# Rebalancing GpSimd's triangular inverse over four steps and moving two short scans, in a gated delta-rule layer

## The reference, cut to what matters

```python
qkvz = hidden_states @ W_qkvz
...
conv = sum((xp[:, j:j + Tv, :] * conv_w[:, j] for j in range(CONV_K)))   # 4 taps
conv = _silu(conv)
...
def step(S, inp):
    q_t, k_t, v_t, a_t, b_t = inp
    S = S * a_t[..., None, None]
    err = jnp.einsum('bhkv,bhk->bhv', S, k_t)
    v_new = (v_t - err) * b_t[..., None]
    S = S + k_t[..., None] * v_new[..., None, :]
    o = jnp.einsum('bhkv,bhk->bhv', S, q_t)
    return (S, o)
...
og = o * _silu(z)
og = og * jax.lax.rsqrt(jnp.mean(og * og, axis=-1, keepdims=True) + EPS) * norm_weight
return og.reshape(Bv, Tv, VDIM) @ W_out
```

## Time and profile before

| | us |
|---|---|
| median of 3 runs (lowest to highest) | 1186.12 (1184.61 to 1191.84) |
| the profiled execution's own time | 1186.36 |
| its span | 1184.6 |
| PE busy | 1085.0 (92%) |
| DVE busy | 931.3 (79%) |
| ACT busy | 801.6 (68%) |
| POOL busy | 740.0 (62%) |
| mean granted PE clock | 0.973 |

### The profile page before, as it was taken

The page is one execution under the profiler, slowest core; times in us unless marked ns, Lnnn a source line. Parts: engine busy times, 40 slices in busy tenths (PEclk is TensorE's granted clock), DMA queues, the critical chain, the costliest instruction groups (busy, mean ns, idle before and its releaser), DMA issues. The chain is left out here.

```text
span 1184.6 us, 29919 instructions
## 1 busy us (share of the span) xinstructions
PE 1085.0 (92%) x10488; PEld 950.3 (80%) x10488; DVE 931.3 (79%) x2531; ACT 801.6 (68%) x2225; POOL 740.0 (62%) x1183
## 2 busy tenths in 40 slices
PE   7885999999999999999999999999989878998985
PEld 6784898889888888988888989888878767776653
DVE  6898798999999898989899999999872534328754
ACT  6442687777777787877777777778675764229883
POOL 3166778787878778787878787877867412015111
PEclk9778899999999999999999999999998999999998
DMA  5222227314040413222231404041224130010000
GB/s 190 66 61 49 76 58 70 89 38 119 15 110 18 111 39 86 56 70 60 69 89 38 118 15 111 17 109 22 61 45 123 35 107 1 1 62 16 2 19 19
DMA packets 140869, 72.79 MB, mean 61 GB/s; under 512 B 114184, under 2 KB 130064, under 8 KB 138800
## 3 DMA queue, kind: packets, MB, share of 16 engines
q1 hardware_dynamic: 140720, 70.88, 23.9%
HBM read 57.06 MB, written 13.78 MB: 60 GB/s over the span
## 5 line engine op out<-in xcount | busy, mean ns | idle before, releaser
L1084 POOL TENSOR_TENSOR Tn<-Tn,tmp 64x31 f32<-64x31 f32 (+15 forms) x496 | 279.3, 563 | 38.9
L1081 POOL TENSOR_TENSOR tmp<-DT,Tn 64x31 f32<-64x31 f32 (+15 forms) x496 | 251.5, 507 | 50.6 <-DMA DT<-blk_in_scratch 11.9
L878 DVE SCALAR_TENSOR_TENSOR cv<-bank,cw,cv 128x255 f32<-128x255 f32 (+2 forms) x384 | 155.0, 472 | 42.2 <-ACT cv L674 41.6
L878 DVE SCALAR_TENSOR_TENSOR cqk<-bank,cw,cqk 128x255 f32<-128x255 f32 (+2 forms) x384 | 154.8, 471 | 35.3 <-ACT cqk L674 35.3
L1052 POOL TENSOR_TENSOR ro<-ss,mhalf 128x4 f32<-128x4 f32 x64 | 72.4, 1132 | 143.5 <-issue 75.9
L935 DVE SCALAR_TENSOR_TENSOR BP<-bank,cj,E 128x512 f32<-128x512 f32 (+1 forms) x256 | 144.5, 610 | 2.5 <-DVE cj L916 0.3
L485 PE MATMUL bank<-wo,OTs 128*128 128x256 f32 x512 | 137.3, 396 | 1.5 <-ACT OTs L767 1.5
L744 ACT ACTIVATE ogn<-og,ro 128x128 f32<-128x128 f32 x256 | 82.1, 401 | 38.8 <-POOL ro L1052 38.8
L736 ACT ACTIVATE junk<-og 128x129 f32<-128x129 f32 x256 | 79.4, 310 | 36.9 <-issue 25.9
L485 PEld LDWEIGHTS bank<-wo,OTs 128*128 128x128 f32 x512 | 89.5, 192 | 13.9 <-ACT OTs L767 2.0
L464 PE MATMUL bank<-Y,BP 128*128 128x128 f32 x512 | 88.6, 275 | 0.1
(11 more groups left out here) (212 smaller groups left out, 3256.1 us busy)
## 6 DMA issues: line engine op xcount, KB each, us to landing
rvz<-in_L_attn_W_qkvz SPq DMA_DIRECT2D x16, 512.0 KB, 5.4
x<-alpha_scratch SPq DMA_DIRECT2D x8, 1024.0 KB, 5.0
alb<-alpha_scratch SPq DMA_DIRECT2D x7, 1024.0 KB, 5.0
rqk<-in_L_attn_W_qkvz SPq DMA_DIRECT2D x16, 256.0 KB, 2.6
wo<-in_L_attn_W_out SPq DMA_DIRECT2D x16, 256.0 KB
blk_in_scratch<-BP SPq DMA_DIRECT2D x256, 16.0 KB, 1.5
DT<-blk_in_scratch SPq DMA_DIRECT2D x16, 256.0 KB, 3.4
tinv_scratch<-Tn SPq DMA_DIRECT2D x32, 128.0 KB, 2.2
```

Of the source, the lines that this page charges most:

```text
L878: nc.vector.scalar_tensor_tensor(d, bk[:, t * T:(t + 1) * T - s], cw[p][:, first + t, TAPS - 1 - s:TAPS - s], d, ALU.mult, ALU.add).then_i ...
L1081: pool_step_done(nc.gpsimd.tensor_tensor(t, D[:, j, j + 1:BLK].unsqueeze(2).broadcast_to([SLOTS, r, c]), T[:, j, 0:c].unsqueeze(1).broadca ...
L1084: pool_step_done(nc.gpsimd.tensor_tensor(T[:, j + 1:BLK, 0:c], T[:, j + 1:BLK, 0:c], t, ALU.subtract), t_rows(kh, j + 1))
```

## The change

Two edits, both in the loop. POOL's 31 rows are dealt 14, 3, 7, 7 over the four steps in place of 16, 3, 7, 5: rows 14 and 15 leave step 0, and step 3 ends with rows 24 to 30 in place of 26 to 30. On DVE, in step 2, the two short scans (L892) move from in front of the q/k taps to behind them, which is in front of the v taps; the long scan stays in front. (From here on lines in the changed kernel are 2 higher: L1081 becomes L1083.)

```diff
                     elif b == 2:
-                        scans_ahead(1, 1)
+                        scans_ahead(1, 1, R)
                 for taps in (taps_v, taps_qk) if merges(b) else (taps_qk, taps_v):
                     for n in range(1, TAPS):
                         taps(n)
+                    if b == 2 and taps == taps_qk:
+                        scans_ahead(1, R)
...
-            SPLIT = ((0, 16), (16, 19), (19, 26), (26, BLK - 1))
+            SPLIT = ((0, 14), (14, 17), (17, 24), (24, BLK - 1))
```

## The result

| | before | after |
|---|---|---|
| median (lowest to highest), us | 1185.55 (1184.61 to 1191.84), 4 runs | 1212.19 (1210.81 to 1213.38), 4 runs |
| ratio, 95% interval | | 1.021 (1.018 to 1.025) |
| profiled execution: own time, span | 1186.36, 1184.6 | 1210.81, 1209.1 |
| mean granted PE clock there | 0.973 | 0.954 |

The account below looks back on a forecast made before the run. PE was the first suspect, with the chain to `UT` arriving at about the same time. Gains of 1.85 against later v side, inverse and landing gave +0.2 a round, +3 us in 13 rounds: 1189 us, range 1176 to 1203.

Parts of the forecast that it names:

- edit 1 up to PE: Rows 14 and 15 leave step 0, so `ogn` starts 1.85 us earlier and PE's wait at L475 goes almost entirely.
- the sum for a round: From one L409 to the next: +0.28 us in odd rounds, +0.15 in even ones, mean +0.2.
- My 1.08 less 0.40: Transposed inverse issued 1.08 us sooner behind the first issue, less 0.40 for slower landing of `UT` when issues crowd.
- The rivals with faster blocks: Blocks keep up, both PE waits go: 1160 us, chance 0.11; or landings as short as the median: 1179, chance 0.15.
- The one with throughput: DMA traffic fixes the time from first issue to `UT` landing: about +1.0 us a round, 1200 us, chance 0.18.
- edit 2: Short scans behind the q/k taps in step 2: PE's wait at L333 goes, v taps and squares of step 2 come later.
- my two terms: Delay of the v side in step 2 from moving the scans: 0.37 us in odd rounds, 0.94 in even ones.
- The step that failed: PE, ready some 2 us earlier each round, waits that long for the blocks at L399 or L409.
- A second step: The gain in front of L475 was counted in rounds 1 to 13 only; the first and last two got none.
- 1.16 us: In step 3 the transposed inverse leaves this much later, seen from the squares of step 2, after the later last row.

Follow-up runs that it names:

- edit 1 alone: Kernel before with POOL's rows dealt 14, 3, 7, 7 and the short scans left in front of the q/k taps: 1196.15 us, ratio 1.010.
- the best dealing: Kernel before with POOL's rows dealt 15, 4, 7, 5, one row moved from step 0 to step 1: 1167.96 us, ratio 0.987.
- the two fillers: Changed kernel with ten useless matmuls a round before the wait for `U`: 1207.90 us; with eight more before the wait for `UT`: 1203.03 us.
- edit 2 alone: Kernel before, dealing 16, 3, 7, 5 kept, with step 2's two short scans moved behind the q/k taps: 1192.37 us, ratio 1.006.
- raw blocks last: Changed kernel with SP's read of raw blocks moved behind the transposed inverse out: 1212.09 us, ratio 1.024 to the kernel before.

## Why the prediction was wrong

**Right: edit 1 up to PE.** `ogn` starts 1.17 behind the squares (I said within 1.3), and the wait at L475 has left the list (under 8). The last row came 7.51 behind the squares (7.5), the transposed inverse 1.55 behind the first issue (1.5 to 1.7), and PE's waits at L399 and L409 are 25.8 (15 to 35). The rounds without a fall are 0.1 longer, where the sum for a round gave 0.2. The reads of `UT` started 5.0 behind the first issue on the median, where it had been 5.6. My 1.08 less 0.40 gave 0.68 for that gain. The rivals with faster blocks fall by the waits. The one with throughput was met at its point in half of the rounds (reads at 5 us or more), but its price of 1.0 a round didn't come.

**Half right: edit 2.** The wait at L333 shrank from 2.4 to 0.5. The delay of the v side was sized wrong. I had 0.37 in odd and 0.94 in even rounds. From the squares of step 1 to those of step 2 it was 11.47 to 11.52 in rounds 1 to 13, where edit 1 alone has 10.97 to 11.00 from round 2 on. So the delay was 0.5 in odd and even rounds alike. (The kernel before has 11.0 in most rounds and 11.49 in the odd ones from 5 to 13.) The delay reaches the round nearly in full: rounds without a fall take 55.06 with both edits and 54.61 with edit 1 alone, and on the dealing 15, 4, 7, 5 edit 2 adds 0.55. The silu of v waits 1.23 for `cv` in round 7, as I said it would wait longer. Its price, 8 us alone and 7 on the best dealing, is near what my two terms come to over 13 rounds (0.65 on the mean, 8.5 in all).

**The step that failed** is the sentence "PE itself would be ready some 2 us earlier in each round, and waits that long for the blocks". I took the 2 us at L475 and the 2 us at the merges for the same 2 us. As idle time they are. But the sum has no term for PE's clock. The waits at L475, of at most 1.8 us, were met at full clock in every round from 1 to 12 of the kernel before. Of the waits at the merges, five in eleven rounds were followed by a stretch at half the clock, which cost 2.3 us each, 11.4 of the 24.5 us.

That the clock matters is shown in three ways: the windows, the two fillers, and the spread of one kernel with its clock. The last gives a second size. A straight line through the 37 executions of the kernel before that were measured beside the experiments has 6.5 us for 0.01 of clock, and one through the ten of edit 2 alone has 7.0. The change took the median clock from 0.970 to 0.951, so by my estimate 12 to 13 us of the loss go with the clock, over all rounds. That is about half of the loss. The rest has other causes, of which round 14 below is one.

What brings the falls shows if all twelve traces are read together. Rounds 2 to 12 hold 17 falls. Each begins inside a wait of PE of 1.26 us or more or within 2.2 us behind its end, and the three dealings with no such wait in these rounds (15, 4, 7, 5; 14, 4, 8, 5; 15, 4, 8, 4) have none. But most such waits bring no fall. At the merges 15 of 39 waits of 1.25 us or more did. At L475 it was none of nine waits of 1.7 to 1.8 us in the kernel before, and two of four of 1.98 to 1.99 us with edit 2 alone. So the falls are a chance that such waits bring. The place seems to matter, since shorter waits do it at the merges, but the merges aren't needed. The executions that weren't profiled agree: the four kernels with 21 to 26 us of waits at L399 and L409 (changed, raw blocks last, edit 1 alone, 16, 3, 5, 7) have median clocks of 0.948 to 0.962, and the kernel before and the three dealings just named 0.967 to 0.970. What decides a single fall stays open.

The Trainium skill (TensorE: Matmul & The Clock Gate, section "HAM oscillation — how this bites in real kernels") warns of idle gaps of PE longer than any in the loop of the changed kernel. The trace differs: in its rounds 2 to 12, waits of 1.5 us at the longest were enough.

**A second step** was the bracket "in the first one and in the last two other things are late". I used it to give these rounds no gain, and also gave them no cost. Rounds 0 and 14 cost 2.8 and 5.1 us (the 2.8 may be scatter, with the -2.3 ahead of it), and round 1, which I had counted as a gain, 3.1: 11.0 of the 24.5 us in all. In round 14 ACT has no later work to do while it waits for the last row. Its turn waits 2.71 us there, for which the kernel before has 0.41:

```profile
953.22 1.17 ACT L761 ACTIVATE DT<-Tn 64x512 f32<-64x512 f32 x1 [2.71 <-POOL Tn L1086]
```
```profile
933.65 1.10 ACT L761 ACTIVATE DT<-Tn 64x512 f32<-64x512 f32 x1 [0.41 <-POOL Tn L1084]
```

The first row is of the changed kernel, the second of the one before. The silu of v, the squares and `hT` are queued behind the turn, and PE waits for `hT` (2.6 us, 1.2 before). The last row is 8.53 behind the squares of step 2 there, where it was 5.46, so it is 3.1 us later, and from L399 to L399 the round grew by 3.1 us. From that L399 to L409 another 2.3 went, since a fall lies there. It begins 0.4 us behind the wait for `hT` (the clock was 0.50 from 957.7 to 964.5):

```profile
957.70:964.50 6.80, 6.29 (x85) 5.52 (x85) 0.00 (x0) 3.07 (x7) 0.15 (x1) 0.50 0.34 54
```

So the later last row, of which I had 1.16 us reaching the end in a normal round, is paid in full where nothing covers it.

**A path that the sum left out.** I followed only the transposed inverse to `UT`. `U` has a shorter way and stands earlier in PE's list (L399). Its reads gained 0.9 behind the first issue (3.5 to 2.6) of the 2.24 by which this issue came later, so it lost 1.3 and became the block that PE waits for in all 13 rounds. The time of a round hardly changed by that, but the idle time stands in front of L399 as well as of L409.

**What stays open.** Round 1 is 3.1 us longer without a fall in it, and takes 62 us with one in two of the experiments. I did not find the cause.

**What the rows of before would have told.** My sum had the price of the rows at their new place (2.24 late at the last row) and the gain at the old one (1.85), and found them about equal. That already spoke against the dealing 14, 3, 7, 7 and for one which leaves step 3 alone: 15, 4, 7, 5 then gave 16 of the 23.4 us of the L475 row.

## What to carry to other kernels

When work is dealt over stages, price where it arrives as well as where it leaves. A row moved out of one step is only a gain if it doesn't come to stand in front of a chain that already arrives just in time, and here the shortest move that cured the wait (one row, one step on) was the best of those tried. Idle time of PE that moves from one place to another needn't cost the same: look at the granted clock behind the waits at both places, and count the first and last rounds apart, where a late item has no cover.

## What the runs showed of the hardware

- PE's clock fell to 0.5 for stretches such as 397.9 to 404.7 us of the changed kernel although PE was busy for 53.3 of the 54.7 us of the round before. The only idle time just before was a wait of 1.26 us, followed by 32x32 matmuls.
- In edit 2 alone it fell twice behind waits of 1.98 and 1.99 us in front of 128x128 transposes. Nine waits of 1.7 to 1.8 us at the same place in the kernel before brought no fall.
- A round with a fall took 57.34 us on the mean, one without 55.06. Ten executions of one kernel (edit 2 alone) were spread over 13.5 us (1184.14 to 1197.61), the clock going from 0.976 to 0.961.
- Eighteen added matmuls of 128x256 a round took the changed kernel from 1212.19 to 1203.03 us and its median clock from 0.951 to 0.975, while the rounds without a fall grew from 55.06 to 55.80.
- The reads of `U` started 2.7 behind the issue of the DMA that they depend on, with the raw blocks issued between them or not.
